# Diffusion over edges of a graph: four accumulation tables in turn in place of three

## The reference, cut to what matters

```
h = relu(layernorm(x));  h = h @ W.T + b
deg[n] = 1 + number of edges with src == n;   dis = 1/sqrt(deg)
agg[n] = dis[n]*dis[n]*h[n] + sum over edges with src == n of dis[n] * dis[dst] * h[dst]
x = x + h + 0.05*(agg - h) + 1.5*relu(h)
```

## Time and profile before

| | |
|---|---|
| median of 3 runs | 6703.62 us |
| the three runs | 6703.62, 6705.91, 6689.98 us |
| the profiled execution, its own time | 6689.26 us |
| its span, first to last instruction | 6686.7 us |
| mean granted clock of TensorE | 0.847 of full speed |
| setup | 0 to 64.8 us |
| degree count: clearing issued at 64.8, next stage's first load | 64.8 to 257.2 us |
| dense part | to 659.8 us |
| additions of the edge stage, first to last start | 697.66 to 1581.46 us |
| closing pass, first load to the next stage's first instruction | 1590.8 to 1846.2 us |

### The profile page before, as it was taken

One profiled execution on the slowest core, in us unless ns is written; L12 is line 12 of the kernel. 1 busy time (PEld: TensorE's weight loads), 2 busy tenths in 40 slices (PEclk: granted clock), 3 DMA queues, 4 the chain that ended last, 5 costly groups with the idle time before them and its releaser, 6 DMA issues. The chain is left out here.

```text
span 6686.7 us, 96995 instructions
## 1 busy us (share of the span) xinstructions
PE 4387.0 (66%) x29194; PEld 3836.3 (57%) x29194; DVE 4362.3 (65%) x5674; ACT 1837.6 (27%) x2782; POOL 3774.4 (56%) x3348
## 2 busy tenths in 40 slices
PE   6665434772068878566665867776787756865887
PEld 3454334662067877555555855555786745755775
DVE  7898554224767777788898842234988955862458
ACT  5643112331033344333333421121453410000001
POOL 0398665773077757777753777773000047757757
PEclk8766667996588999877778988898999978988899
DMA  6398776667955557533334855454678851231109
GB/s 240 89 275 263 157 151 142 142 140 231 414 179 167 170 173 259 169 96 103 99 106 135 269 181 140 139 159 125 215 253 299 309 191 42 58 124 14 14 11 306
DMA packets 865593, 1128.43 MB, mean 169 GB/s; under 512 B 591583, under 2 KB 604276, under 8 KB 864060
## 3 DMA queue, kind: packets, MB, share of 16 engines
q1 hardware_dynamic: 409660, 807.13, 36.1%
q10 hardware_dynamic: 311296, 226.11, 11.1%
q0 software_dynamic: 144256, 90.12, 9.2%
HBM read 633.88 MB, written 495.44 MB: 169 GB/s over the span
## 5 line engine op out<-in xcount | busy, mean ns | idle before, releaser
L897 POOL DMA_INDIRECT gc_msgs<-t,src_rows x784 | 755.0, 963 | 1120.6 <-POOLq L148 826.4
L2080 PE MATMUL gc_ring<-gc_msgs,gc_hot 128*128 x4736 | 654.3, 297 | 232.0 <-SPq L2039 231.1
L2080 PEld LDWEIGHTS gc_ring<-gc_msgs,gc_hot 128*128 128x128 f32 x4736 | 627.7, 210 | 307.2 <-issue 299.7
L951 POOL DMA_INDIRECT acc<-de_sums,de_put x392 | 607.7, 1550 | 311.5 <-issue 157.9
L897 POOL DMA_INDIRECT edge_rows<-h,dst_rows x392 | 378.6, 966 | 231.8 <-issue 116.1
L897 POOL DMA_INDIRECT at1s_ends<-x,src_rows x392 | 403.2, 1028 | 158.5 <-issue 118.3
L897 POOL DMA_INDIRECT edge_rows<-x,dst_rows x392 | 384.5, 981 | 166.9 <-issue 116.1
L897 POOL DMA_INDIRECT re_rows<-x,src_rows x392 | 404.4, 1032 | 125.2 <-issue 124.3
L1503 PE MATMUL re_psR<-w_rel,re_own 128*128 128x128 f32 x3136 | 402.5, 295 | 69.8 <-DVE re_own L1440 69.5
L897 POOL DMA_INDIRECT at2s_ends<-h,src_rows x392 | 370.0, 944 | 127.4 <-issue 118.7
L1503 PEld LDWEIGHTS re_psR<-w_rel,re_own 128*128 128x128 f32 x3136 | 395.4, 210 | 78.2 <-issue 75.3
(11 more groups left out here) (539 smaller groups left out, 11235.7 us busy)
## 6 DMA issues: line engine op xcount, KB each, us to landing
rew_win<-x SPq DMA_DIRECT2D x74, 544.0 KB
at1w_win<-g SPq DMA_DIRECT2D x74, 544.0 KB
at2w_win<-g SPq DMA_DIRECT2D x74, 544.0 KB, 4.1
de_win<-t ACTq DMA_DIRECT2D x74, 512.0 KB, 4.6
de_near<-same SPq DMA_DIRECT2D x74, 512.0 KB, 5.0
x<-rew_win SPq DMA_DIRECT2D x74, 512.0 KB
h<-at1w_win SPq DMA_DIRECT2D x74, 512.0 KB
h<-at2w_win SPq DMA_DIRECT2D x74, 512.0 KB, 2.9
```

Source lines behind the costliest of these rows:

```text
L897: nc.gpsimd.indirect_dma_start(buf[:, t * width:(t + 1) * width], None, table, bass.IndirectOffsetOnAxis(ap=rows[:, t:t + 1], axis=0)).the ...
L951: nc.gpsimd.indirect_dma_start(g.acc0[j % LANES], bass.IndirectOffsetOnAxis(ap=put[:, j:j + 1], axis=0), sums[:, j * D:(j + 1) * D], None, ...
L2080: done = nc.tensor.matmul(ring[:, bass.ds(to[n], SLOT)], hot[k][:, n, :], each_group(msgs[:, bass.ds(of[n], MID)], SLOT // MID), start=Fal ...
```

## The change

A fourth table `acc03` is made, and group j of the edge stage uses table j mod 4 and waits for group j - 4. The fourth table is cleared in `setup` (spare tiles) and in `out_degrees` (the rest), right behind the third. In `diffusion_close` each chunk has a fourth load and a third addition.

```
--- before.py
+++ after.py
@@ -55,7 +55,7 @@
 EPS = 1e-5
 assert NP >= N
 AHEAD = 33
-LANES = 3
+LANES = 4
 
 
 class Batch:
@@ -129,7 +129,7 @@
 
 
 DMA_SIGNALS = {"loaded", "weights", "attrs", "zeroed", "o_stored", "x_in", "stored", "got", "ea_in", "seam_got", "seam_put", "last_in", "last_out", "path_put", "path_in", "line_put", "src_in", "same_put", "same_in", "ahead", "win_in", "acc_in", "done_out", "base_in", "types_in",
-               ("de", "added0"), ("de", "added1"), ("de", "added2"), ("deg", "blanked_lane"), ("re", "blanked_rows"), ("dd", "cleared")}
+               ("de", "added0"), ("de", "added1"), ("de", "added2"), ("de", "added3"), ("deg", "blanked_lane"), ("re", "blanked_rows"), ("dd", "cleared")}
 
 
 class Room:
@@ -698,9 +698,10 @@
         with nc.Block() as block:
             @block.sync
             def _(sp):
-                sp.dma_start(g.acc0[2].rearrange("(p t) d -> p (t d)", t=PITCH)[:, 0:TILES * D].rearrange("p (c w) -> p c w", w=1024),
-                             each_group(g.zeros[:, :], TILES * D // 1024)).then_inc(blanked_lane, 16)
-                sp.wait_ge(blanked_lane, 16)
+                for lane in g.acc0[2:]:
+                    sp.dma_start(lane.rearrange("(p t) d -> p (t d)", t=PITCH)[:, 0:TILES * D].rearrange("p (c w) -> p c w", w=1024),
+                                 each_group(g.zeros[:, :], TILES * D // 1024)).then_inc(blanked_lane, 16)
+                sp.wait_ge(blanked_lane, 32)
 
             @block.gpsimd
             def _(pool):
@@ -1129,7 +1130,7 @@
 
     W = J * D
     with Room(nc, g, "dc") as r:
-        base, acc, third = ([r.sb(f"{n}{k}", [P, W]) for k in range(SLOTS)] for n in ("base", "acc", "third"))
+        base, acc, third, fourth = ([r.sb(f"{n}{k}", [P, W]) for k in range(SLOTS)] for n in ("base", "acc", "third", "fourth"))
         tiny = r.sb("tiny", [P, COLS])
         x_in, stored = ([r.sem(f"{n}{k}") for k in range(SLOTS)] for n in ("x_in", "stored"))
         free, link_s, ready = (r.sem(n) for n in ("free", "link", "ready"))
@@ -1143,6 +1144,7 @@
                     sp.dma_start(base[b.slot][:, :], chunk_of(g.acc0[1], b.number)).then_inc(x_in[b.slot], 16)
                     sp.dma_start(acc[b.slot][:, :], chunk_of(g.acc0[0], b.number)).then_inc(x_in[b.slot], 16)
                     sp.dma_start(third[b.slot][:, :], chunk_of(g.acc0[2], b.number)).then_inc(x_in[b.slot], 16)
+                    sp.dma_start(fourth[b.slot][:, :], chunk_of(g.acc0[3], b.number)).then_inc(x_in[b.slot], 16)
                 pipeline(sp, load, slots=SLOTS)
 
             @block.vector
@@ -1153,9 +1155,10 @@
                 def close(b):
                     s = b.slot
                     link.restart()
-                    dve.wait_ge(x_in[s], 48 * b.nth)
+                    dve.wait_ge(x_in[s], 64 * b.nth)
                     link(nc.vector.tensor_tensor(base[s][:, :], base[s][:, :], acc[s][:, :], ALU.add))
                     link(nc.vector.tensor_tensor(base[s][:, :], base[s][:, :], third[s][:, :], ALU.add))
+                    link(nc.vector.tensor_tensor(base[s][:, :], base[s][:, :], fourth[s][:, :], ALU.add))
                     nc.vector.tensor_tensor(grouped(base[s][:, :], D), grouped(base[s][:, :], D), spread(tiny[:, bass.ds(b.number * J, J)], D), ALU.mult).then_inc(ready, 1)
                 pipeline(dve, close, slots=SLOTS)
```

## The result

The change makes the kernel slower: 6741.47 us (median of 4 runs, 6740.37 to 6750.48) against 6697.81 us (4 runs, 6689.98 to 6705.91). The ratio is 1.0068 with a 95% interval of 1.0051 to 1.0085. That is +44 us by the medians, +52.8 us between the two profiled executions (6742.01 against 6689.26). The prediction had added up +55.6 us and forecast 6753 us, in a range from 6735 to 6780.

A forecast was written before the change was run, and what follows sets the result against it. The prediction saw a row of stages with different limits, the closing pass bound by DMA bytes. Setup +1.3, degree count 0, edge stage -9.2 and closing pass +63.5 made +55.6 us on the 6697.2 mean: forecast 6753, range 6735 to 6780.

The forecast's parts named there:

- The sum: Whole kernel: setup +1.3, degree count 0, edge stage -9.2 and closing pass +63.5 make +55.6 us, forecast 6753 us.
- the stages behind the closing pass: After 1846 us: no term in the sum; a rival at 0.05 had them change, with 17 us allowed either side.
- Setup: Clearing one more table's spare tiles puts 512 KB on SP's queue ahead of the path's transfers: +1.3 us.
- Degree count: The second clearing of 25.7 MB lands near 194 us, covered by the stage's other work: 0, bounds 0 and +2.
- Closing pass: A stream of bytes: the fourth table's 25.7 MB cost 62.2 us, the last chain's add 1.3, together +63.5 us.
- Rival B: Closing pass held by its four slots, not bytes: +31 there, +24 in total, 6721 us; chance 0.05.
- Edge stage: POOL's last batch starts at 1559.3 instead of 1568.50, just behind ACT's last copy: stage ends 9.2 us earlier.
- the last 51 blocks: Edge stage after 1124 us: PE and ACT take 433.6 us, 8.5 each, and a faster POOL does not hurry them.
- The waits: POOL's edge-stage waits on landings fall from 96.1 to under 15 us; those for ACT grow to 100 or more.
- Rival A: Edge stage gains nothing, as landings lengthen or producers come later: +64.8, 6762 us; chance 0.12.
- Rival C: Additions' waits are the whole edge stage's path: all 70 us go, total -5, 6692 us; chance 0.03.
- The rule of the Trainium skill: Edge-stage additions land some 3.6 us after issue, so none waits on three tables; sum 9.2 us higher.

The follow-up runs named there:

- e4: The kernel before with four tables cleared in the degree count in place of one: 6741.4 us against 6685.3, one run of each.
- e1: The kernel after, its edge stage using only three of the four tables in turn, the fourth still cleared and added: 6759.47 us against 6695.1, ratio 1.0093.
- e8: The kernel after without the closing pass's fourth load, the third table's chunk added twice instead: closing pass 258.5 us against 255.8.
- e6: The kernel before with all 392 additions of the edge stage left out: edge stage 873.1 us, copies 837.1 us.
- e10: The kernel before (three tables) with DVE's compare of the next batches moved ahead of its wait for PE's sums: 6629.24 us against 6685.52, ratio 0.9913.
- e9: The kernel before with two of its three tables in turn in the edge stage, the third still cleared and added: edge stage 1048.8 us.
- e11: The kernel after (four tables) with DVE's compare moved ahead of its wait for PE's sums: 6609.25 us, ratio 0.9885.

## Why the prediction was right, point by point

- *The sum*: 6753 us forecast, 6741.47 measured, +55.6 against +44. Stage by stage it came nearer, +53.6 between the spans, and that is partly luck: the edge stage gave 7.2 us more than its term, and the stages behind the closing pass, which the sum had at 0, took 4.9 us more.
- *Setup*, +1.3: measured +1.7, by the mechanism named. SP's L412 starts at 48.0 to 48.6 us in the six profiles without a fourth table, at 49.5 to 50.1 in the five with it, and at 50.7 in that with five tables. The whole stage spreads more, 63.0 to 64.8 us without and 64.4 to 66.9 with it.
- *Degree count*, 0: right. The second clearing landed at 194 us, as worked out, and e4 shows what covers it and how much more it would cover.
- *Closing pass*, +63.5: measured +63.2, and 63.1 in e1. Bytes at one rate; e8 leaves no more than 3 us to the add. Rival B is out.
- *Edge stage*, -9.2: measured -16.4, the one term that was off. Over the profiles it is -12.3 (edge stages of 918.5 to 934.4 us with three tables, 914.1 to 916.6 with four or five). What the term was made of held: POOL's lag at the end gave 8.6 us here (23.7 to 15.1), and 8.2 over the profiles (mean of four with three tables 23.3, of four with more 15.0). The reason given for it held only nearly. In all four of those profiles with more tables the last batch waits for POOL's batch before it and starts 0.5 us later than the last copy would allow, so that POOL's pace and the last copy all but tie. The rest is ahead of the last copy: 2.8 us to the first copy, which was chance, and 5.6 us between the copies. I had written of the last 51 blocks that a faster POOL does not hurry them, and from block 25 on that is so (410.1 and 410.4 us). The blocks before that I had put at nothing, and there e6 shows that the additions do touch the producers. Whether four tables change this stays open: the copies took 854.6 to 864.4 us with three tables (mean 861.1) and 856.1 to 858.7 with four or five (mean 857.1), so the 4 us of difference lie inside the spread of three. The fastest, 853.8, is that with two tables, whose additions are the most spread out.
- *The waits*: 6.6 us on landings (under 15 said), 148.9 on ACT (100 or more). Rival A, no gain, is out by e1 against the kernel after and by the stage lengths. Rival C needed 70 us from waits that mostly turned into waits for ACT.
- The rule of the Trainium skill ("DMA: Bandwidth & Descriptors", section "Anatomy of one DMA — SWDGE (gpsimd) path"), by which nothing would have waited on three tables, does not agree with e10 either, which has 120.5 us in 89 waits. e9 does not decide: the 3.6 us of landing estimated by that rule are more than the 2.95 us that two tables leave free. The median landings of 3.4 to 4.4 us lie near the 3.6; what makes the waits is the long ones, up to 8.4 us (e11).
- The stages behind the closing pass differ by +4.9 us; over the profiles they range from 4839 to 4855 us with no order by tables, so this is spread. The +44 us by medians and the +53.6 by spans differ mostly by the kernel before, whose profiled execution was 8.6 us faster than its median and whose runs lie between 6674.61 and 6711.64 us.

## What to carry to other kernels

A wait removed from an engine that runs behind its producers is worth only that engine's lag at the end: read the last producer's date and the consumer's last start, before adding up waits. A table more in rotation costs its bytes in every pass over it that nothing else covers, here 25.7 MB at 410 GB/s, and that price is sure while the gain hangs on who is late next. So look first for what holds the producers; with them freed, the same fourth table went from 44 us slower to 20 us faster.

## What was not expected of the hardware

The store of 256 KB and the load of 512 KB that the producers wait for take longer with the small additions beside them than without: the store's wait 4.8 against 3.1 us in one block, the medians by 0.3 and 0.4 us. This happens while the DMA engines are not full, at a share of 0.68 before and 0.48 in e6 (the last but one column, in this order):

```profile
...
700.00:1120.00 420.00, 168.84 (x1064) 153.56 (x1065) 209.60 (x300) 66.47 (x106) 271.61 (x175) 0.67 0.68 148
```

```profile
...
700.00:1110.00 410.00, 178.72 (x1117) 163.36 (x1118) 209.65 (x303) 69.66 (x111) 0.00 (x0) 0.68 0.48 141
```

Such a share did not mean room for a chain that waits for each transfer's landing.
